# Attention with stacked high and low halves, moved weight splits, and grouped edge strips

## Chip, core and metric

The kernel runs on one core of a Trainium2 chip. The metric is the device time of one launch in microseconds (us), as the median of several runs. TensorE (PE), VectorE (DVE), ScalarE (ACT), GpSimd (POOL) and the DMA queues work from queues of their own, in order, and meet at semaphores.

## What is computed

Two graph layers over 625 nodes of width 768, with 10000 edges. The change touches three parts: the edge counts, and the linear attention of either layer.

```python
# layer 0, no softmax: q, k, v from xn @ W_qkv + b_qkv, 12 heads of 64
phi_q = relu(einsum('bhnd,md->bhnm', q, random_features))     # 256 features
phi_k = relu(einsum('bhnd,md->bhnm', k, random_features))
kv = einsum('bhnm,bhnd->bhmd', phi_k, v)
attn = einsum('bhnm,bhmd->bhnd', phi_q, kv) / 256
# layer 1
phi(t) = exp(einsum('bhnd,md->bhnm', t, random_features) - 0.5 * sum(t * t)) / 16
out = einsum('bhnm,bhmd->bhnd', q_p, kv) / (einsum('bhnm,bhm->bhn', q_p, k_sum) + 1e-6)
# edges, sorted by dst: how many of each type lead from a node to a node
count[src, dst] += BASE ** edge_type
```

All products are made in float32 accuracy from pairs: a value is held as high (rounded to fp32r) and low (the rest), and a product is the sum of two or three matmuls.

## The kernel before

The program is a row of phases, each a block with one instruction list for each engine, and a barrier behind it. `phase_start` (0 to 68 us in the trace) loads the input, counts the edges and normalises x. `phase_attend` is the attention, called as m0 (68 to 288 us) and, with `second` true, as m1 (1103 to 1347 us). Between and behind them stand graph convolutions, a feed-forward layer and the mixture of experts (from about 1500 us), which the change leaves as they are.

**The edge counts.** The 10000 edges are 80 tiles of 125. For tile n, `hot(n)` makes on DVE a one-hot matrix of the sources (`src_hot`, 125x640, L1204) and one of the destinations (`dst_hot`, L1206), which holds only a window of 96 columns, since the edges are sorted; the latter carries the weight of the edge type. TensorE multiplies them into PSUM (L1289, about six matmuls a tile). `src_hot` has 16 slots (UNROLL). DVE makes 24 tiles, then the statistics and the normalised x, and then the other 56. From tile 44 on, TensorE turns a piece of x every third tile (`turn`, L1273, ten pieces, all through bank 7): ACT copies the piece as high half (L1257), DVE subtracts for the low half (`low`, L1213), and only then the next piece may be turned. When all tiles are done, ACT and DVE copy the counts out of PSUM.

**The weight ring.** Weights arrive in chunks in a ring of two slots. `ring_high` (ACT, L128) rounds a chunk of 128x1536, `ring_low` (DVE, L139) makes the low half, and only then the slot of raw data takes the next load.

**The attention.** It begins with the values of all heads (`values`, L179), each tile of which DVE adds a bias to in m0 (L703), and the first pair's projection. Then a loop over six pairs of heads. For pair p TensorE does, in this order:

- `features_k`: five tiles of keys (t), each three matmuls of 512 columns (high*high, high*low, low*high) against `rfbd`, the random features of both heads in a block diagonal, and behind each tile one of twelve units of the next pair's projection (`project_unit`, L187, six matmuls of 314 columns; units 0 to 5 make keys, 6 to 11 queries). In m1 two further matmuls a tile subtract the squares (L477).
- `features_q`: four tiles of queries (m), six matmuls of 314 columns each, and behind each a unit. In m1 four more a tile.
- `keys_values` (L520), 40 matmuls; units 9 to 11; `attend`, 24 matmuls.

ACT makes the high half of each feature tile (L628, L641), DVE the low half (L747, L755; L745, L753 in m1). Tile t of the keys waits for the low half of tile t-2 in m0 and for the high half in m1, since they share a bank; so do the query tiles. `qk_high` and `qk_low` split the projected keys and queries, 128x628 at a time. The keys of the next pair are split behind the first query tile. At the end of a pair's pass stand, on ACT and DVE, the split of a ring chunk, in m0 the addition of `b_proj` to x (L788), and in m1 the reciprocal of the denominators, 128x628 on DVE (L781), and the product with it.

## Time and profile before

| what | us |
|---|---|
| median of 3 runs (2268.36 to 2272.95) | 2268.71 |
| the profiled execution | 2272.92 |
| its span | 2271.2 |
| DVE busy (58% of the span) | 1313.0 |
| PE busy (91% of the span) | 2067.2 |
| ACT busy (39% of the span) | 888.4 |

Busy time is the time in which an engine has an instruction under way. The profiled execution lies 4.2 us above the median. In the page's 40 slices of 56.8 us, PE is at five tenths in the first slice and at seven to nine in the next four, which are the start and the first attention.

### The profile page before, as it was taken

How to read it: one execution, taken by the hardware profiler on the slowest of the kernel's cores; microseconds unless marked ns; L12 is line 12 of the kernel's file. 1: busy time of each engine (PE TensorE's matmuls, PEld its weight loads, DVE VectorE, ACT ScalarE, POOL GpSimd, SP SyncE). 2: the span in 40 equal slices, each digit the busy share in tenths (PEclk: the TensorE clock that was granted, in tenths of full speed). 3: DMA queues.
4: the chain of work that ended last, by engine and by line, in shares of the span. 5: the costliest groups of instructions: out<-in, count | busy, mean ns of one | idle time of the engine just before them, and what ended most of it. 6: DMA issues, size and time to landing. Idle time of an engine off the chain costs nothing. (4 is left out here: it accounts for less than half of the span.)

```text
span 2271.2 us, 34213 instructions
## 1 busy us (share of the span) xinstructions
PE 2067.2 (91%) x13755; PEld 1941.2 (85%) x13755; DVE 1313.0 (58%) x1909; ACT 888.4 (39%) x1079; POOL 90.5 (4%) x60
## 2 busy tenths in 40 slices
PE   5799889999999999974799979699979999999996
PEld 4788879999999999974789979699978888888885
DVE  9444466433243434355545555663258888898896
ACT  1233331211111211211255542221237777777775
POOL 0000000000000000000010100000000110101001
PEclk8899989999999999986799988899989999999998
DMA  2310026210221111101210021231259999999997
GB/s 65 100 43 29 1 78 151 66 41 25 66 66 50 45 63 55 45 15 28 91 29 29 15 84 63 79 123 63 77 189 388 385 377 379 364 373 378 363 378 269
DMA packets 186157, 313.72 MB, mean 138 GB/s; under 512 B 12641, under 2 KB 86884, under 8 KB 185628
## 3 DMA queue, kind: packets, MB, share of 16 engines
q1 hardware_dynamic: 178844, 294.53, 36.9%
q0 software_dynamic: 4816, 16.62, 3.1%
q8 instruction: 88, 1.44, 0.3%
q10 hardware_dynamic: 2384, 0.92, 0.2%
q14 instruction: 25, 0.20, 0.0%
HBM read 293.56 MB, written 20.40 MB: 138 GB/s over the span
## 5 line engine op out<-in xcount | busy, mean ns | idle before, releaser
L179 PE MATMUL psum<-re_whi,xt_sb 128*128 128x512 f32 (+1 forms) x1680 | 507.9, 377 | 1.5 <-DVE xt_sb L2716 1.5
L179 PE MATMUL psum<-ring_hi,xt_sb 128*128 128x256 f32 (+3 forms) x1980 | 371.5, 286 | 14.1 <-DVE a_sb L703 6.0
L179 PEld LDWEIGHTS psum<-re_whi,xt_sb 128*128 128x128 f32 x1680 | 313.3, 189 | 46.7 <-issue 1.9
L179 PEld LDWEIGHTS psum<-ring_hi,xt_sb 128*128 128x128 f32 (+1 forms) x1980 | 314.1, 191 | 15.6 <-DVE a_sb L703 6.8
L2700 DVE TENSOR_TENSOR re_wlo<-moe_raw,re_whi 128x1536 fp32r<-128x1536 f32 x173 | 303.5, 1756 | 35.2 <-ACT re_whi L2654 34.5
L179 PE MATMUL psum<-re_wlo,xt_sb 128*128 128x512 f32 (+1 forms) x840 | 313.6, 373 | 0.0
L2654 ACT ACTIVATE re_whi<-moe_raw 128x1536 fp32r<-128x1536 f32 x174 | 258.6, 1489 | 91.0 <-PE psum L179 87.6
L179 PE MATMUL psum<-ring_lo,xt_sb 128*128 128x256 f32 (+3 forms) x990 | 281.9, 285 | 0.0
L179 PEld LDWEIGHTS psum<-ring_lo,xt_sb 128*128 128x128 f32 (+1 forms) x990 | 189.4, 191 | 0.0
L179 PEld LDWEIGHTS psum<-re_wlo,xt_sb 128*128 128x128 f32 x840 | 159.1, 189 | 21.9
L128 ACT ACTIVATE ring_hi<-ring_raw 128x1536 fp32r<-128x1536 f32 (+2 forms) x67 | 102.3, 1526 | 176.7 <-PE psum L187 81.4
L139 DVE TENSOR_TENSOR ring_lo<-ring_raw,ring_hi 128x1536 fp32r<-128x1536 f32 (+2 forms) x67 | 121.8, 1818 | 75.7 <-ACT ring_hi L128 66.1
L2700 DVE TENSOR_TENSOR re_wlo<-re_more,re_whi 128x1536 fp32r<-128x1536 f32 x84 | 147.6, 1758 | 29.7 <-ACT re_whi L2654 29.7
L179 PE MATMUL psum<-ring_hi,gnn_sb 128*128 128x256 f32 (+1 forms) x810 | 150.6, 287 | 7.2 <-PEq L1308 4.2
L2654 ACT ACTIVATE re_whi<-re_more 128x1536 fp32r<-128x1536 f32 x84 | 125.2, 1490 | 41.3 <-PE psum L179 37.6
L187 PE MATMUL psum<-xt_sb,ring_hi 128*128 128x314 f32 x744 | 140.7, 312 | 0.0
L1458 DVE TENSOR_TENSOR g_y<-psum,g_y 128x256 fp32r<-128x256 f32 (+3 forms) x105 | 42.4, 405 | 167.8 <-ACT g_y L1425 167.6
L179 PEld LDWEIGHTS psum<-ring_hi,gnn_sb 128*128 128x128 f32 (+1 forms) x810 | 127.4, 190 | 9.0 <-issue 7.8
L1425 ACT ACTIVATE g_y<-psum 128x256 fp32r<-128x256 f32 (+3 forms) x105 | 38.6, 368 | 232.1 <-PE psum L179 232.1
L187 PEld LDWEIGHTS psum<-xt_sb,ring_hi 128*128 128x128 f32 x744 | 119.8, 192 | 4.7
L1401 PE MATMUL psum<-gnn_sb,g_y 128*128 128x314 f32 (+1 forms) x780 | 117.1, 308 | 0.0
L179 PE MATMUL psum<-ring_lo,gnn_sb 128*128 128x256 f32 (+1 forms) x405 | 115.6, 285 | 0.0
(391 smaller groups left out, 3282.8 us busy)
## 6 DMA issues: line engine op xcount, KB each, us to landing
moe_raw<-in_L_ffn_Wg_r SPq DMA_DIRECT2D x74, 768.0 KB, 8.6
moe_raw<-in_L_ffn_Wu_r SPq DMA_DIRECT2D x58, 768.0 KB, 8.3
moe_raw<-in_L_ffn_Wd_r SPq DMA_DIRECT2D x42, 768.0 KB, 6.0
re_more<-in_L_ffn_Wd_r SPq DMA_DIRECT2D x42, 768.0 KB, 9.2
re_more<-in_L_ffn_Wu_r SPq DMA_DIRECT2D x30, 768.0 KB, 7.6
ring_raw<-in_L_gnn_w_rel SPq DMA_DIRECT2D x18, 896.0 KB, 5.0
re_more<-in_L_ffn_Wg_r SPq DMA_DIRECT2D x15, 768.0 KB, 7.1
ring_raw<-in_L_mix_W_qkv SPq DMA_DIRECT2D x24, 384.0 KB, 4.3
```

The source lines that it names most:

```text
L128: act.activation(ring.hi[:, g % RING_SLOTS, 0:size], ring.raw[:, g % RING_SLOTS, 0:size], ACT.Copy).then_inc(ring.hi_done, 1)
L139: dve.tensor_tensor(lo, raw, hi.bitcast(F32), ALU.subtract).then_inc(ring.lo_done, 1)
L179: mm = pe.matmul(out, lhs[a], rhs[b], start=(first and i == 0), stop=(last and i == 2))
L187: mm = pe.matmul(bank_pair[:, h, 0:HN], lhs[a], rhs(b, h), start=(first and i == 0), stop=(last and i == 2))
L1401: mm = pe.matmul(pair[:, h, 0:HN], y[0:TS[t], v % 2, t, a, m * P:(m + 1) * P], k.C[0:TS[t], r, t, h * HN:(h + 1) * HN], start=(t == 0 and ...
L1425: act.activation(y[0:TS[t], v % 2, t, 0, 0:w], k.banks[i % 3][0:TS[t], 0:w], ACT.Copy).then_inc(s["y_hi"], 1)
L1458: dve.tensor_tensor(y[0:TS[t], v % 2, t, 1, 0:w], k.banks[i % 3][0:TS[t], 0:w], y[0:TS[t], v % 2, t, 0, 0:w].bitcast(F32), ALU.subtract).t ...
L2654: act.activation(whi[:, slot, :], raw[i % RAWS], ACT.Copy).then_inc(s["hi_done"], 1)
L2700: dve.tensor_tensor(wlo[:, i % RING, :], raw[i % RAWS], whi[:, i % RING, :].bitcast(F32), ALU.subtract)\
```

## The change

**Stacked halves.** `qk` gets a slot for each head. For head hd the partitions of that head hold the high half, and the other 64 partitions hold the low half of the same head. `rf2` holds the features twice, one below the other, as high (index 0) and low (index 1), 256 columns each. A matmul over 128 partitions then sums high and low of q or k at once. A key tile takes four matmuls of 256 columns, a query tile four of 314. `qk_high` and `qk_low` are two instructions of 64 partitions each where one of 128 stood.

**Order in a pair's pass.** Unit 5 goes ahead of the query tiles, and so does the split of the next keys. The ring's split goes from the end of a pass to behind the query tiles of the next one, and with it in m0 the addition of `b_proj`. In m1 the reciprocal of pair p-1 is made in four parts of 157 columns behind the first four key tiles of pair p, and the product follows the split of the keys; the wait for the squares stands ahead of a key tile.

**The start.** `phase_start` loads the three biases and the features for m0, behind chunk 0. The destination one-hots are made for eight tiles in one `tensor_tensor` (125x768, window starts on a straight line for eight tiles, from POOL's iota), and the weight goes to the source side. Every fourth source one-hot is made on ACT, in two steps: |column - source|, and relu(weight - weight * that).

```diff
-            bv = k.sb(f"{name}_bv", [P, D], F32)
-            bq = k.sb(f"{name}_bq", [P, 2 * PAIRS], F32)
-            bp = k.sb(f"{name}_bp", [P, D], F32)
+            bv, bq, bp = k.v_bias, k.qk_bias, k.out_bias
...
-                    mm = split_product(pe, out, [qk[:, KEYS, a, t * P:t * P + TS[t]] for a in range(2)],
-                                       [rfbd[:, a, :] for a in range(2)], True, not second)
+                    for hd in range(2):
+                        out = key_bank(t)[:, hd * MF:(hd + 1) * MF]
+                        for a in range(2):
+                            mm = pe.matmul(out, qk[:, KEYS, hd, t * P:t * P + TS[t]], rf2[:, a, :],
+                                           start=(a == 0 and not second), stop=(a == 1 and (hd == 1 or not second)))
                     mm.then_inc(s["pk_mm"], 1)
                     project_unit(p + 1, t)
+                project_unit(p + 1, TT)
...
-                    mm = split_product_wide(pe, pair, [rfbd[:, a, m * P:(m + 1) * P] for a in range(2)],
-                                            lambda b, h: qk[:, QUERIES, b, h * HN:(h + 1) * HN], True, not second)
+                    hd, e = divmod(m, 2)
+                    for a in range(2):
+                        for h in range(2):
+                            mm = pe.matmul(pair[:, h, 0:HN], rf2[:, a, e * P:(e + 1) * P],
+                                           qk[:, QUERIES, hd, h * HN:(h + 1) * HN],
+                                           start=(a == 0), stop=(a == 1 and not second))
...
+                for hd in range(2):
+                    src, dst = qk_pair[a][own(hd), :, 0:HN], halves(qk[own(hd), a, hd, :])
...
+                if p + 1 < PAIRS:
+                    qk_high(p + 1, KEYS)
                 for m in range(4):
...
-                    if m == 0 and p + 1 < PAIRS:
-                        qk_high(p + 1, KEYS)
...
+                if p >= 1 and p + 5 <= len(st.chunks):
+                    ring_high(act, st, p + 5)
                 act.wait_ge(s["kv_mm"], p + 1)
...
-            if not second:
-                dve.wait_ge(s["bias_in"], 32)
...
+                    if second and p >= 1 and t < 4:
+                        quarter = den[:, t * (NT // 4):(t + 1) * (NT // 4)]
+                        if t == 0:
+                            dve.wait_ge(s["den_f"], 2 * p)
+                        ins = dve.reciprocal(quarter, quarter)
...
+                if p + 1 < PAIRS:
+                    qk_low(p + 1, KEYS)
+                if second and p >= 1:
+                    normalise(p - 1)
...
+GROUP = 8
+ON_ACT = [n for n in range(ET) if n % 4 == 3]
...
+            def strips(g):
+                at = slice(g * GROUP, (g + 1) * GROUP)
+                columns = iota[0:EP, 0:WINDOW].rearrange("p (o w) -> p o w", o=1).broadcast_to([EP, GROUP, WINDOW])
+                places = within[:, at].rearrange("p (j o) -> p j o", o=1).broadcast_to([EP, GROUP, WINDOW])
+                dve.tensor_tensor(dst_hot[:, at, :], columns, places, ALU.is_equal).then_inc(s["strip"], 1)
...
+                act.activation(away[:, i % 2, :], iota[0:EP, :], ACT.Abs, bias=minus[:, 0, n:n + 1]).then_inc(s["away"], 1)
+                act.wait_ge(s["away"], i + 1)
+                act.activation(src_hot[:, n % UNROLL, :], away[:, i % 2, :], ACT.Relu, bias=weight[:, 0, n:n + 1],
+                               scale=minus[:, 1, n:n + 1]).then_inc(s["act_hot"], 1)
```

How the instructions stand on DVE in m0, before, over one pass of a pair (p = 1: L747 is the low half of key tiles, L755 of query tiles, L718 the low half of the projected keys or queries, L139 the ring):

```order
L747 SCALAR_TENSOR_TENSOR m_phik<-psum,m_phik 113x512
L755 SCALAR_TENSOR_TENSOR m_phiq<-psum,m_phiq 128x628
L718 SCALAR_TENSOR_TENSOR m_qk<-psum,m_bq,m_qk 128x628
L755 SCALAR_TENSOR_TENSOR m_phiq<-psum,m_phiq 128x628 x3
L766 SCALAR_TENSOR_TENSOR m_kvf<-psum,m_kvt 128x2x64 x2
L773 TENSOR_TENSOR m_kv<-m_kvf,m_kv 128x512
L718 SCALAR_TENSOR_TENSOR m_qk<-psum,m_bq,m_qk 128x628
L139 TENSOR_TENSOR ring_lo<-ring_raw,ring_hi 128x1536
L788 TENSOR_TENSOR x_sb<-x_sb,m_bp 128x768
L747 SCALAR_TENSOR_TENSOR m_phik<-psum,m_phik 128x512 x4
```

The same place on DVE in the changed kernel (L752 key tiles, L771 query tiles, L720 projected keys or queries):

```order
L752 SCALAR_TENSOR_TENSOR m_phik<-psum,m_phik 113x512
L720 SCALAR_TENSOR_TENSOR m_qk<-psum,qk_bias,m_qk 64x628 x2
L771 SCALAR_TENSOR_TENSOR m_phiq<-psum,m_phiq 128x628 x4
L139 TENSOR_TENSOR ring_lo<-ring_raw,ring_hi 128x1536
L777 TENSOR_TENSOR x_sb<-x_sb,out_bias 128x768
L784 SCALAR_TENSOR_TENSOR m_kvf<-psum,m_kvt 128x2x64 x2
L791 TENSOR_TENSOR m_kv<-m_kvf,m_kv 128x512
L720 SCALAR_TENSOR_TENSOR m_qk<-psum,qk_bias,m_qk 64x628 x2
L752 SCALAR_TENSOR_TENSOR m_phik<-psum,m_phik 128x512 x4
```

The ring and the addition have gone from ahead of the key tiles to behind the query tiles, and the split of the next keys from behind the first query tile to ahead of it.

DVE in m1 of the changed kernel, from the numerators of pair 0 (L797) to the query tiles of pair 1 (L750 key tiles, L758 the reciprocal, L726 the product with it):

```order
L797 COPY a_sb<-psum 64x628 x2
L750 TENSOR_TENSOR m_phik<-x_sb,m_phik 128x512
L758 RECIPROCAL x_sb<-x_sb 128x157
L750 TENSOR_TENSOR m_phik<-x_sb,m_phik 128x512
L758 RECIPROCAL x_sb<-x_sb 128x157
...
L750 TENSOR_TENSOR m_phik<-x_sb,m_phik 113x512
L718 TENSOR_TENSOR m_qk<-psum,m_qk 64x628 x2
L726 TENSOR_TENSOR a_sb<-a_sb,x_sb 128x628
L769 TENSOR_TENSOR m_phiq<-x_sb,m_phiq 128x628 x4
L139 TENSOR_TENSOR ring_lo<-ring_raw,ring_hi 128x1536
```

And before:

```order
L779 COPY a_sb<-psum 64x628 x2
L781 RECIPROCAL x_sb<-x_sb 128x628
L783 TENSOR_TENSOR a_sb<-a_sb,x_sb 128x628
L139 TENSOR_TENSOR ring_lo<-ring_raw,ring_hi 128x1536
L745 TENSOR_TENSOR m_phik<-x_sb,m_phik 128x512 x4
```

The reciprocal, the product and the ring all stood ahead of the first key tile; now one part of the reciprocal stands behind each of the first four.

## Rows read from the trace of the kernel before

**Rows 1.** Stretches: us, busy time (instructions) per engine, granted clock, DMA share, GB/s
```profile
178.90:264.50 85.60, 78.73 (x527) 75.67 (x526) 36.83 (x49) 30.79 (x48) 0.00 (x0) 0.98 0.06 19
1183.80:1311.40 127.60, 123.34 (x805) 115.65 (x805) 72.38 (x84) 71.88 (x120) 12.40 (x8) 1.00 0.06 19
```

**Rows 2.** Timeline, DVE, first tiles: start us, us, engine, line, operation [idle before]
```profile
6.74 0.39 DVE L1204 TENSOR_SCALAR n_src_hot<-n_iota,n_edges_f 125x640 bf16<-125x640 f16 x1
7.04 0.30 DVE L1206 TENSOR_SCALAR n_dst_hot<-n_iota,n_edges_f,n_edge_weight 125x96 bf16<-125x96 f16 x1
7.26 0.38 DVE L1204 TENSOR_SCALAR n_src_hot<-n_iota,n_edges_f 125x640 bf16<-125x640 f16 x1
```

**Rows 3.** Timeline, start, where x is turned between edge tiles
```profile
57.08 0.63 PE L1273 MATMUL psum<-ident,n_xn 128*128 128x128 f32 x4 [0.77 <-DVE xt_sb L1213]
...
57.74 0.60 ACT L1257 ACTIVATE xt_sb<-psum 128x512 fp32r<-128x512 f32 x1 [1.70 <-PE psum L1273]
...
58.37 0.69 DVE L1213 TENSOR_TENSOR xt_sb<-psum,xt_sb 128x512 fp32r<-128x512 f32 x1
...
59.21 0.41 PE L1273 MATMUL psum<-ident,n_xn 128*128 128x128 f32 x2 [0.83 <-DVE xt_sb L1213]
...
64.43 0.40 DVE L1213 TENSOR_TENSOR xt_sb<-psum,xt_sb 128x226 fp32r<-128x226 f32 x1
```

**Rows 4.** Timeline, the first values of m0
```profile
79.08 1.76 DVE L139 TENSOR_TENSOR ring_lo<-ring_raw,ring_hi 128x1536 fp32r<-128x1536 f32 x1 [9.37 <-DMA m_bq<-in_L_mix_b_qkv]
...
81.23 0.58 PE L179 MATMUL psum<-ring_hi,xt_sb 128*128 128x256 f32 x1 [5.81 <-DVE a_sb L703]
...
81.61 0.42 PE L179 MATMUL psum<-ring_lo,xt_sb 128*128 128x256 f32 x1
...
82.25 0.41 PE L179 MATMUL psum<-ring_lo,xt_sb 128*128 128x256 f32 x1
...
85.06 0.28 PE L179 MATMUL psum<-ring_lo,xt_sb 128*128 128x256 f32 x1
...
85.42 0.28 PE L179 MATMUL psum<-ring_lo,xt_sb 128*128 128x256 f32 x1
```

**Rows 5.** Timeline, PE and DVE in passes of m0
```profile
163.04 1.04 PE L187 MATMUL psum<-m_qk,m_rfbd 128*128 128x314 f32 x6
...
164.79 1.04 PE L187 MATMUL psum<-m_qk,m_rfbd 128*128 128x314 f32 x6
...
168.30 4.58 PE L520 MATMUL psum<-m_v,m_phik 128*128 128x130 f32 x40
...
178.95 0.85 PE L179 MATMUL psum<-m_rfbd,m_qk 128*128 128x512 f32 x3
...
179.64 0.74 PE L187 MATMUL psum<-xt_sb,ring_hi 128*128 128x314 f32 x4
...
181.25 1.76 DVE L139 TENSOR_TENSOR ring_lo<-ring_raw,ring_hi 128x1536 fp32r<-128x1536 f32 x1 [3.98 <-ACT ring_hi L128]
...
182.93 0.95 DVE L788 TENSOR_TENSOR x_sb<-x_sb,m_bp 128x768 f32<-128x768 f32 x1
...
184.53 0.96 PE L179 MATMUL psum<-m_rfbd,m_qk 128*128 128x512 f32 x3 [2.30 <-DVE m_phik L747]
```

**Rows 6.** The tile m_qk: duration in ns, least/median/most, first and last start
```profile
L587 ACT ACTIVATE m_qk<-psum,m_bq x12: 783/785/787, 106.0 to 261.2; 128x628 fp32r<-128x628 f32 x12
L718 DVE SCALAR_TENSOR_TENSOR m_qk<-psum,m_bq,m_qk x12: 871/872/875, 106.8 to 262.0; 128x628 fp32r<-128x628 f32 x12
L583 ACT ACTIVATE m_qk<-psum x12: 693/696/702, 1132.6 to 1307.7; 128x628 fp32r<-128x628 f32 x12
```

**Rows 7.** Timeline, passes of m1: reciprocal, and waits of the key tiles
```profile
1184.77 4.08 DVE L781 RECIPROCAL x_sb<-x_sb 128x628 f32<-128x628 f32 x1
...
1188.57 0.96 PE L179 MATMUL psum<-m_rfbd,m_qk 128*128 128x512 f32 x3 [0.59 <-ACT m_phik L628]
...
1319.17 0.95 PE L179 MATMUL psum<-m_rfbd,m_qk 128*113 128x512 f32 x3 [1.88 <-ACT m_phik L628]
```

203 lines of the change are left out of this document (127 added, 76 removed).

## The prediction

> **What bounds the kernel now.** I read the busy time by stretches first, to see which engine sets the pace where the change works, and then the timeline of one pass. In both attention loops it is PE: three passes of the first attention (m0) take 85.6 us with PE busy for 78.7, four of the second (m1) 127.6 us with PE busy for 123.3, while DVE and ACT are busy for little over half of that at most [rows 1]. So a matmul taken away there is worth its time, and in m0 PE's idle time, 2.3 us a pass, is worth more still. The timeline says what it waits for: the third key tile waits for the low half of the first (at 184.53) [rows 5], and DVE made that late, since the ring's split (from 181.25) and the addition of b_proj (182.93) stood ahead of it. The start is another matter. There DVE works without a gap on one-hots, and PE waits for it. A tile costs DVE 0.30 us for the source part and 0.22 for the window (the starts at 6.74, 7.04 and 7.26) [rows 2], 0.52 together. And m0 begins with a hole: PE idles for 5.81 us until DVE has taken the first values away, DVE having waited 9.37 us for a bias to land [rows 4].
>
> **The start.** DVE's work for the tiles: 60 source parts at 0.30 are 18.0 us, and ten strips of 768 elements. No row has such a strip. The nearest is the addition of two 128x768 tiles, 0.95 us (at 182.93) [rows 5]; neighbours on DVE overlap by some 0.08 us (the 1.76 us at 181.25 are followed after 1.68), so ten strips cost 8.7 us. Bounds: 3 us, were a strip no dearer than a source part of nearly the same size, and 12, were broadcast operands dear. Before, the tiles took 80 x 0.52 = 41.6 us; now 26.7. But the end of this stage does not follow DVE alone. From tile 44 on there is a chain over ten pieces of x: PE turns (57.08), ACT copies 0.66 later, DVE subtracts 0.63 later, PE turns the next 0.84 later [rows 3], 2.1 us for a large piece and by the smaller shapes about 1.5 for a small one. It went at (64.43 - 58.37) / 3 = 2.0 us a piece, with one-hots in between. Now ACT also has 20 source parts to make, of two dependent instructions each. The nearest rows are activations of 628 elements, 0.70 us without a bias read per partition and 0.79 with one [rows 6]; the first step has one such operand and the second two, so 0.80 + 0.88, some 1.7 us a tile. Eight of them fall among the ten pieces. ACT's copies take 5 x 0.60 + 5 x 0.38 (the latter scaled down from 512 to 256 elements) = 4.9 us, the eight tiles 13.6, and for the two pieces that have no tile ahead of them the chain shows, about 2.5: 21 us from the first piece to the last one-hot, against 9 x 2.0 + 1 before. So nothing is gained behind tile 44, and perhaps 2 us lost. Ahead of it ACT is not late: it makes six tiles while DVE makes the first 24, and the rest while DVE does the statistics. DVE gains there on 24 + 29 tiles: 53 x 0.52 = 27.6 us before, 40 x 0.30 + 7 x 0.87 = 18.1 now, less 0.5 for four small instructions ahead of the first tile. In all 27.6 - 18.1 - 0.5 - 2 = 7, and since the last tiles no longer wait for DVE, I take **8 us** (3 to 13). The four small loads stand on SP's queue ahead of chunk 1, which nobody needs for 40 us. POOL's ten iotas stand ahead of the identity matrix; at a tenth of a microsecond each they are hidden behind the edges' landing, and I leave them in the range.
>
> The Trainium skill speaks against giving ACT this work. ScalarE: Activation LUTs, in its Rules for kernel authors, says to put relu and its like on VectorE, which is faster per element in bf16. The rows agree as to the price, 0.30 us against an estimated 1.7, and what counts here is only whose queue is free.
>
> **The hole at the head of m0.** With the bias there beforehand, DVE takes the values as they come and PE does not stop: 5.8 us. Behind the hole the clock was low. Three matmuls of 256 columns took 0.64 us at 81.61 and 0.36 at 85.06 [rows 4], which is the step from the level of 1.2 GHz to that of 2.4, and this lasted from 81.2 to 84.4: half of 3.2 us, 1.6. **7.5 us** (5.5 to 9). The memory transfers that the next chunks need begin as before, at the barrier; the ring is not the cover of anything new.
>
> **m0, a pass.** A key tile's three matmuls of 512 columns took 0.69 us (178.95 to 179.64). Four of 256 take 4 x 0.118 = 0.47 [rows 4]: 0.22 less, 1.1 for five tiles. A query tile with its unit took 1.75 us for twelve matmuls of 314 columns (163.04 to 164.79), 0.146 each; two less in each of four tiles is 1.2. Together **2.3 us**. Should matmuls of 256 columns cost as much as those of 314, the weights being changed each time, the key tiles would gain only 0.5. The wait of 2.3 us goes, since the ring and the addition now stand where DVE waits for the 4.4 us of `keys_values` (168.30) anyway: ACT's part of the split and then 1.7 + 0.9 on DVE end about when PE is through, so this cover is just wide enough; were it not, the remainder would fall on the path up to `attend`. With the wait goes a part of the clock's dips (0.98 in the mean) [rows 1], 0.8 a pass. What is late next: the query tiles. Unit 5 done, ACT makes two high halves of 0.79, and DVE then two low halves of 0.87, at which only it starts on the low half of query tile 0 (another 0.8). That is 0.2 + 1.5 + 1.6 + 0.8 = 4.1 us behind unit 5. PE does two query tiles with their units in 2 x (4 x 0.146 + 0.875) = 2.9 and then needs it: a new wait of **1.3 us**, in five passes, where it had none. It is bounded by 0.5 (if neighbours overlap more than I take) and 1.8. A pass gains 2.3 + 2.3 + 0.8 - 1.3 = 4.1. Four such passes give 16.4. The first one had another wait, on the ring split ahead of the loop, which stays and even grows as PE is sooner there: 0.6. The last has no units to fill the gaps and is paced by DVE: 1.0. **m0's loop: 18 us** (13 to 24).
>
> **m1, a pass.** The same 2.3 from the matmuls. The waits are smaller: 0.59 us for the third key tile (at 1188.57) [rows 7], and (127.6 - 123.3) / 4 = 1.1 in all [rows 1]. The ring's conversion on ACT, which caused the 0.59, goes behind the query tiles; I give 1.0 for the waits. Doubling the splits costs nothing here, as PE waits in m1 for high halves only. DVE is the one to watch: a quarter of the reciprocal is 4.08 / 4 = 1.02 us and a key tile 0.65 (0.87 for 628 elements [rows 6], scaled to 512, less the overlap), together 1.7, against PE's 0.47 + 2 x 0.23 + 0.875 = 1.8 for a key tile with its unit. It just fits. Four passes: 4 x 3.3 = 13.2. The first, which had no wait, gains 1.9. The last has nothing to hide behind; DVE's 4.08 in one piece made PE wait, once for 1.88 us [rows 7], and in quarters it will wait less: 2.0 (0 to 4). Ahead of the loop the split of the queries now takes ACT and DVE 0.6 and 0.7 us longer and PE already waits there: -0.9. **m1: 16 us** (10 to 20).
>
> **The sum.** 8 + 7.5 + 18 + 16 = 49.5 us. The profiled execution took 2272.9, which gives 2223.4; it lies 4.2 above the median of the three runs, and so I forecast 2268.7 - 49.5 = 2219. The rest of the kernel stands behind barriers and is moved as a whole.
>
> **Rivals.** (a) DVE becomes the bound in m1. If a quarter costs 1.3 us rather than 1.02, a key tile costs DVE 2.0 against PE's 1.8; ACT waits for the low half two tiles back, PE for ACT, and a pass loses 0.2 x 5 and the waits that I struck, 1.8 in all. Over five passes 9 us: 2228. For it: DVE is at 57% of m1's passes already and gets 1.4 us more a pass. Against: the reciprocal's time goes with its elements. (b) The start gains nothing, since ACT's one-hots hold the chain (2.5 us a tile instead of 1.7 would do): 2227. (c) More is gained: the new wait in m0 is absent because the instructions overlap, the last passes and the start are at the good end of their ranges: 9 us more, 2210. (d) Slower. PE's clock fell to the low level around the 5.81 us hole and in m0's passes of which the wait was 2.3 (0.98). If the new wait at the third query tile, 1.3 us, let it fall there and it stayed so to the end of the pass, then 2.9 + 4.4 + 2.6 + 3.5 = 13.4 us of matmuls would take twice as long, 67 us over five passes: 2286, 0.8% slower. From a cost of 10 us a pass on this decides the sign. Against it: after a wait as long as 2.3 us the mean clock was still 0.98.
>
> TensorE: Matmul & The Clock Gate, in the Trainium skill, describes under HAM oscillation a kernel that idled for a transfer in every step and started each step at the low clock; that is mechanism (d), which this trace shows behind a hole of 5.8 us and barely in the passes.
>
> **How the numbers follow.** The forecast, within 2213 to 2225: 52%. (a) 16%, (b) 11%, (c) 19%, (d) 2%. The range must reach (a), (b) and (c) with their spread: 2207 to 2231. A measurement of this kernel can tell 0.2% from no change, 4.5 us. Faster by more than that is all but (d) and a little beside it: 97%; within it 1%; slower 2%.
>
> **What would show it.** The strip's and ACT's durations, and the start of the count copies at about 57 us instead of 65.4. No wait of PE at the third tile of m0's values. Key tiles of four matmuls at 0.47 us. In m0 no wait at the third key tile, but one of 1.3 us at the third query tile for DVE's low half. Passes of 24.7 us in m0 and 28.5 in m1. Wrong would be: waits of PE for DVE in m1's key tiles (a), turns more than 2.3 us apart (b), or a clock under 0.9 in the passes (d).

## The result: 38 us faster, 12.6 us above the forecast time

| | before | after | difference |
|---|---|---|---|
| median, us (executions) | 2269.89 (4) | 2231.60 (4) | 38.3 |
| lowest to highest | 2268.36 to 2272.95 | 2230.74 to 2233.24 | |
| ratio, 95% interval | | 0.9830 (0.9813 to 0.9848) | |
| profiled execution / its span | 2272.9 / 2271.2 | 2230.7 / 2229.0 | 42.2 |

The forecast was 2219 (2207 to 2231), so the time came out 12.6 us above the forecast and 0.6 us above the range. The sign was right, the size was not: 49.5 us forecast, 42.2 found between the two profiled executions, 38.3 between the medians. Where the 42.2 come from shows in a table by stages, made from PE's timelines: the first matmul of m0, the first key tile of each pass, the first matmul of the phase behind each attention.

| stage, us | before | after | gain | forecast |
|---|---|---|---|---|
| start, to m0's first matmul | 68.2 | 62.4 | 5.8 | 8 |
| m0 ahead of its loop | 53.8 | 46.4 | 7.4 | 7.5 |
| m0 pass 1 | 27.3 | 28.7 | -1.3 | 0.6 |
| m0 passes 2 to 5 | 115.2 | 99.3 | 15.9 | 16.4 |
| m0 pass 6, to the next phase | 25.8 | 24.7 | 1.1 | 1.0 |
| m1 ahead of its loop | 49.7 | 50.8 | -1.1 | -0.9 |
| m1 pass 1 | 30.9 | 29.5 | 1.4 | 1.9 |
| m1 passes 2 to 5 | 127.6 | 115.1 | 12.5 | 13.2 |
| m1 pass 6, to the next phase | 37.9 | 37.8 | 0.2 | 2.0 |
| all other phases | | | 0.3 | 0 |

Four parts of it are short: the start (2.2 us), m0's first pass (1.9), m1's last pass (1.8) and m1's passes 1 to 5 (1.2). The other 5 us of the 12.6 are in the base: I took a gain worked out on a profiled execution from the median of others, 4.2 us below it, and the profiled execution after the change lies 0.9 below its own median.

The trace of the changed kernel, in the order of the rows shown of before. A stretch answers to each of [rows 1]: us, PE's busy time, granted clock, DMA share, GB/s; first passes 2 to 5 of m0, then pass 6 of m0, passes 2 to 5 of m1, pass 6 of m1.

```profile
137.44:236.72 99.28, 93.74 (x690) 1.00 0.09 25
236.72:261.39 24.67, 15.94 (x102) 0.92 0.02 2
1155.16:1270.26 115.10, 113.09 (x793) 1.00 0.07 21
1270.26:1308.02 37.76, 23.19 (x126) 0.79 0.02 6
```

PE is busy 94% of m0's passes 2 to 5, where it was 92% in [rows 1], and at full clock. Against [rows 2] stand the groups of the start by shape (times, mean ns after the bar): the source one-hots with their second operation, a strip, and the two steps on ACT.

```profile
L1240 DVE TENSOR_SCALAR n_src_hot<-n_iota,n_edges_f,n_edge_weight 125x640 bf16<-125x640 f16 x60 | 22.8, 441 | 0.0
L1247 DVE TENSOR_TENSOR n_dst_hot<-n_iota,n_within 125x768 bf16<-125x768 f16 x10 | 9.5, 951 | 0.0
L1309 ACT ACTIVATE n_src_hot<-n_away,n_edge_weight,n_minus 125x640 bf16<-125x640 f16 x20 | 18.4, 920 | 0.7
L1307 ACT ACTIVATE n_away<-n_iota,n_minus 125x640 f16<-125x640 f16 x20 | 16.3, 817 | 7.4 <-DVE n_minus L1276 5.2 <-PE psum L1367 2.3
```

Against [rows 4 and 5], PE's timeline (start, us, ..., [idle before]): m0's first matmuls with no hole, pass 1, the second pass's first key tile.

```profile
62.38 0.36 PE L179 MATMUL psum<-ring_hi,xt_sb 128*128 128x256 f32 x1 [2.78 <-PEq L1174]
...
63.05 0.60 PE L179 MATMUL psum<-ring_hi,xt_sb 128*128 128x256 f32 x2
...
113.67 0.75 PE L476 MATMUL psum<-m_rf,m_qk 128*128 128x256 f32 x4 [2.06 <-DVE m_phik L752]
114.25 1.22 PE L187 MATMUL psum<-xt_sb,ring_hi 128*128 128x314 f32 x4
...
124.66 0.85 PE L502 MATMUL psum<-m_qk,m_rf 128*128 128x314 f32 x4 [1.38 <-DVE m_phiq L771]
...
137.44 0.64 PE L476 MATMUL psum<-m_rf,m_qk 128*128 128x256 f32 x4
137.91 0.74 PE L187 MATMUL psum<-xt_sb,ring_hi 128*128 128x314 f32 x4
```

A key tile takes 0.47 us (137.44 to 137.91), as forecast, and the wait at the third query tile is 1.38 us, in each of five passes, where 1.3 was forecast. Two things were not priced. At 63.05 the matmuls take longer (the low clock, 63.05 to 66.2). And behind the wait of the third key tile of pass 1, 2.06 us, the next four matmuls take 1.22 us instead of 0.74: the granted clock is 0.57 from 114 to 118 us, where it was 1.00 in the first pass before. DVE's timeline names what is ahead of that key tile:

```profile
111.25 1.76 DVE L139 TENSOR_TENSOR ring_lo<-ring_raw,ring_hi 128x1536 fp32r<-128x1536 f32 x1 [0.95 <-ACT ring_hi L128]
112.93 1.28 DVE L752 SCALAR_TENSOR_TENSOR m_phik<-psum,m_phik 128x512 fp32r<-128x512 f32 x2
```

That is the split of chunk 5, which the change left ahead of the loop. A third thing stands ahead of m0's loop, DVE and PE:

```profile
98.23 1.75 DVE L720 SCALAR_TENSOR_TENSOR m_qk<-psum,qk_bias,m_qk 64x628 fp32r<-64x628 f32 x2 [3.48 <-ACT m_qk L589]
100.02 1.76 DVE L139 TENSOR_TENSOR ring_lo<-ring_raw,ring_hi 128x1536 fp32r<-128x1536 f32 x1
101.81 0.76 DVE L703 TENSOR_TENSOR a_sb<-psum,v_bias 128x256 f32<-128x256 f32 x2
102.29 0.38 PE L179 MATMUL psum<-ring_hi,xt_sb 128*128 128x256 f32 x1 [1.44 <-DVE a_sb L703]
```

PE waits 1.44 us there for values that DVE takes away only behind the split, now of two instructions, and a ring chunk. The kernel before has no such wait. The last pass of m1, against [rows 7], DVE, ACT and PE:

```profile
1277.35 1.12 DVE L758 RECIPROCAL x_sb<-x_sb 128x157 f32<-128x157 f32 x1
...
1278.93 1.12 DVE L758 RECIPROCAL x_sb<-x_sb 128x157 f32<-128x157 f32 x1
1280.09 0.69 DVE L750 TENSOR_TENSOR m_phik<-x_sb,m_phik 113x512 fp32r<-113x512 f32 x1
...
1280.89 0.69 ACT L644 ACTIVATE x_sb<-psum 128x628 f32<-128x628 f32 x1 [2.29 <-DVE m_phik L750]
...
1282.22 1.41 PE L502 MATMUL psum<-m_qk,m_rf 128*128 128x314 f32 x4 [2.14 <-ACT m_phiq L645]
...
1286.58 5.48 PE L526 MATMUL psum<-m_v,m_phik 128*128 128x130 f32 x40
```

The quarters stand between DVE's key tiles, which end at 1280.8; ACT waits 2.29 us for that, PE 2.14 for ACT, and the clock falls behind it (1.41 us for four matmuls that take 0.73 at full clock).

### The profile page after: what moved, and what is told of

It is laid out like the page before. It is cut to its first block and busy times, and to the rows that moved or that the text cites. A ratio compares the mean times of both kernels' runs of the same rounds, so it can differ in the third digit from the quotient of the medians.

```text
span 2229.0 us, 34175 instructions
## 1 busy us (share of the span) xinstructions
PE 2031.5 (91%) x13715; PEld 1919.2 (86%) x13715; DVE 1324.0 (59%) x1860; ACT 940.3 (42%) x1143; POOL 89.9 (4%) x70
## 3 DMA queue, kind: packets, MB, share of 16 engines
q8 instruction: 88, 1.44, 0.3%
## 5 line engine op out<-in xcount | busy, mean ns | idle before, releaser
L139 DVE TENSOR_TENSOR ring_lo<-ring_raw,ring_hi 128x1536 fp32r<-128x1536 f32 (+2 forms) x67 | 121.5, 1813 | 56.2 <-ACT ring_hi L128 56.0
```

What stands on the lines that cost most here:

```text
L139: dve.tensor_tensor(lo, raw, hi.bitcast(F32), ALU.subtract).then_inc(ring.lo_done, 1)
```

## Experiments

Each is timed beside executions of the kernel before, whose median lies between 2268.5 and 2272.4 us from one group of runs to the next, so that the ratios compare better than the times. The stage times are of the profiled execution of each; the profile's stages agree from kernel to kernel within 0.2 us where nothing was changed and the clock is full.

### The three parts alone

Each takes one part of the change into the kernel before: the counts of the start; the four small loads moved to the start; the attention. The fourth is the change whole, once more.

> The kernel before with the new counting of the first stage alone (grouped edge strips, every fourth source one-hot on ScalarE); biases and both attentions are the old ones. Theory (the stages add up): the first matmul of m0 starts near 62.4 instead of 68.1 us and everything behind keeps its length, so the time falls by 5.5 to 6.5 us (ratio 0.9974). Rival (the loads that m0 waits for at its head start in m0 and not earlier, but the weights it streams were asked for in the first stage and now have 6 us less to land): part of the 5.8 us comes back as a longer wait in the first 54 us of m0, and the time falls by only 2 to 4 us.

> The kernel before with the four small loads of m0 (three biases and the random features) moved into the first stage alone. Theory: the hole at the head of m0 goes and nothing else moves: the stretch from m0's first matmul to its first pass falls from 53.8 to about 46.4 us, and the time by 7 to 8 us (ratio 0.9967). Rival (part of the 7.4 us seen in the changed kernel came from its other edits, such as the smaller feature matrix, or the first stage pays for the four loads): under 5 us.

> The kernel before with the new attention alone in both layers (stacked halves, the new order of ScalarE and VectorE, reciprocal in quarters); first stage old, biases loaded in m0. Theory: passes 2 to 5 take 24.8 us each in m0 and 28.8 in m1, a wait of 1.38 us stands at the third query tile of each of the first five passes of m0, the wait of about 2.1 us at the third key tile of m0's first pass is there too, since both come from the order on VectorE; the time falls by 25 to 30 us (ratio 0.988). Rival (the late third key tile of the first pass and the low clock behind it come from the earlier start of m0): pass 1 is 26.8 us or less here against 28.7 in the changed kernel, and the time falls by 28 to 32.

> The changed kernel once more, beside the three parts on one chip. Theory: the three parts make the whole: 0.9974 * 0.9967 * 0.988 = 0.982 of the kernel before. Rival (they interact): the whole differs from the product by over 0.2%. It also tells how the executions of the kernel before scatter about the profiled one, of which about 4 us of the miss are made.

| | median | ratio (95%) | m0 starts | ahead of loop | m0: pass 1, 2 to 5 (mean), 6 | m1: pass 1, 2 to 5, 6 |
|---|---|---|---|---|---|---|
| before | 2269.7 | | 68.2 | 53.8 | 27.3, 28.8, 25.8 | 30.9, 31.9, 37.9 |
| start_only | 2265.6 | 0.9979 (0.9970 to 0.9989) | 62.2 | 54.0 | 27.4, 28.8, 25.8 | 31.0, 31.9, 38.0 |
| bias_only | 2258.2 | 0.9944 (0.9927 to 0.9961) | 68.2 | 43.6 | 27.3, 28.8, 27.0 | 30.9, 31.9, 36.8 |
| attend_only | 2244.8 | 0.9889 (0.9873 to 0.9905) | 69.5 | 55.9 | 28.7, 24.9, 25.4 | 29.5, 28.7, 36.2 |
| same_after | 2232.0 | 0.9826 (0.9811 to 0.9842) | 62.8 | 47.5 | 28.7, 24.8, 25.5 | 29.6, 28.8, 37.7 |

The theory of added stages holds for the start (6.0 us in the trace, 4.1 between medians; the head of m0 keeps its length, so the rival of a longer wait there is out) and the attention (24.9 us; pass 1 has its 28.7 here too, so the rival that the earlier start made it late is out). It fails for the biases: alone they bring 10.3 us ahead of the loop, not 7.4, and 11.5 between medians. The three medians' gains add up to 40.4 us, the whole has 37.7; by the ratios this is 0.9813 for the product and 0.9826 (0.9811 to 0.9842) for the whole, so the times alone don't tell them apart, and the stages have to. Ahead of m0's loop bias_only takes 43.6 us, the changed kernel 46.4, and two things make these 2.8 us. One is the wait of 1.44 us at 102.29: attend_only has it too, 1.44 us, and order_only (below), with the new order but splits of one instruction, does not, so the doubled splits bring it. The other is the clock. PE's stretches show it, 10 us from m0's first matmul on (busy, clock, DMA share, GB/s): before, bias_only, after; then the first 7 us of before and of bias_only.

```profile
68.00:78.00 10.00, 7.24 (x36) 0.67 1.06 292
```
```profile
68.00:78.00 10.00, 9.82 (x83) 1.00 1.03 319
```
```profile
62.00:72.00 10.00, 9.62 (x69) 0.83 1.01 312
```
```profile
68.00:75.00 7.00, 6.82 (x34) 0.55 1.00 299
```
```profile
68.00:75.00 7.00, 6.82 (x57) 1.00 1.00 315
```

So before, the clock was low ahead of the hole as well, and not only behind it, and bias_only gains that too. What lets it be high there is not shown. With the old start it was 0.55 from 68 to 75 us in two profiles, 0.76 in two more, and 1.00 in bias_only alone; with the new start and no matmuls added there, all eleven profiles that have the early biases show 0.50 to 0.64 from 62 to 66 us.

### What the order is worth and what the matmuls

order_only has the new order and the quarters with the old products of three matmuls; old_order is the changed kernel with the old order of ACT and DVE. The core of order_only, on DVE (old_order goes the other way):

```diff
                     ins.then_inc(s["pk_lo"], 1)
...
+                if p + 1 < PAIRS:
+                    qk_low(p + 1, KEYS)
...
                 for m in range(4):
...
-                    if m == 0 and p + 1 < PAIRS:
-                        qk_low(p + 1, KEYS)
+                if p >= 1 and p + 5 <= len(st.chunks):
+                    ring_low(dve, st, p + 5)
...
-                if p + 6 <= len(st.chunks):
-                    ring_low(dve, st, p + 6)
```

> The kernel before with the new order on ScalarE, VectorE and TensorE and the reciprocal in quarters, but with the old feature products of three matmuls (no stacked halves), the old first stage and the biases loaded in m0. Theory (the order takes the waits away, the stacked halves 2.33 us of matmuls from each pass, and in m0 the wait of 1.38 is less here, since the first two query tiles are 0.3 us longer each): passes 2 to 5 take 26.3 to 26.8 us in m0 and 30.5 to 31.2 in m1; against the kernel before the time falls by 10 to 16 us. Rival (the two parts only help together, as the stacked halves did harm with the old order: 29.3 to 34 us a pass in m0 against 28.0 and 29.6 before): passes within 0.5 us of before.

> The changed kernel with the stacked halves but the old order on ScalarE and VectorE: keys of the next pair behind the first query tile, weight split at the end of the pass, reciprocal whole at the end. Theory (of the 4.1 us per pass gained in m0, 2.3 are matmuls and 1.8 the order net of its new wait): passes 2 to 5 of m0 take 26.3 to 26.8 us each, no wait of 1.38 us; those of m1 29.8 to 31.0; the time rises by 10 to 16 us against the changed kernel. Rival (the order brings nothing net, the matmuls and the clock that stays up do it all): within 3 us of the changed kernel.

order_only: 2253.2 us, 0.9921 (0.9905 to 0.9937); passes 2 to 5 take 25.45 to 25.49 us in m0, where I expected 26.3 to 26.8, and 30.5 in m1, with no wait in m0's. old_order: 2255.8 us (2246 to 2272), 0.9930 (0.9910 to 0.9950), 24 us slower than the changed kernel, m0's passes 33.1, 34.0, 29.3, 30.4, 30.5 us in the profiled execution, which is the slowest of its six. I expected 26.3 to 26.8 a pass and a loss of 10 to 16, so both missed. m1's passes came as expected, 30.5 us. With shorter key tiles PE comes to the third one sooner, and the old order makes it wait longer than the old products did: 2.97 us here, 2.30 in [rows 5].

```profile
178.25 1.76 DVE L139 TENSOR_TENSOR ring_lo<-ring_raw,ring_hi 128x1536 fp32r<-128x1536 f32 x1 [2.39 <-ACT ring_hi L128]
179.93 0.95 DVE L791 TENSOR_TENSOR x_sb<-x_sb,out_bias 128x768 f32<-128x768 f32 x1
```
```profile
181.63 0.74 PE L476 MATMUL psum<-m_rf,m_qk 128*128 128x256 f32 x4 [2.97 <-DVE m_phik L752]
182.21 0.93 PE L187 MATMUL psum<-xt_sb,ring_hi 128*128 128x314 f32 x4
...
184.31 1.25 PE L187 MATMUL psum<-xt_sb,ring_hi 128*128 128x314 f32 x4
```

The low clock behind it does the rest (0.93 and 1.25 us for what takes 0.74). So in m0 the stacked halves, 2.3 us of matmuls a pass, bring 0.65 with the new order (25.47 to 24.82). The new wait takes the rest: 1.38 us of idling, and 1.65 with the slower start behind it (172.49 to 175.01 us from one unit to the next at the third query tile, 171.03 to 171.90 at the second). With the old order they do harm in m0 (29.3 to 34.0 us a pass against 28.0 to 29.6 before), but not in m1, where a pass takes 30.5 us against 31.9 before.

### The new wait in m0

q_first puts the keys' low half behind the first query tile on DVE. interleave puts the low half of one head there where it was, and that of the other behind the second query tile, ACT signalling the heads apart:

```diff
-                if p + 1 < PAIRS:
-                    qk_low(p + 1, KEYS)
+                if p + 1 < PAIRS:
+                    qk_low(p + 1, KEYS, range(2) if second else (0,))
...
                     ins.then_inc(s["pq_lo"], 1)
+                    if not second and m == 1 and p + 1 < PAIRS:
+                        qk_low(p + 1, KEYS, (1,))
```

> The changed kernel; on VectorE, in m0 alone, the low half of the first query tile is taken ahead of the low half of the next pair's keys. Theory (the 1.38 us at the third query tile are the two instructions of the keys' low half, which stand ahead of it): the wait goes in all five passes, nothing takes its place, passes 2 to 5 take 23.4 to 23.6 us instead of 24.8, and the time falls by 6 to 7 us against the changed kernel. Rival (ScalarE or the key-value bank is next: it waits for the keys' low half or for the later low halves): a wait of 0.5 us or more appears ahead of the key-value product or at the fourth query tile, and only 2 to 4 us are gained.

> The changed kernel; ScalarE signals the two halves of the split keys apart, and VectorE in m0 takes the low half of one head ahead of the first query tile and that of the other behind the second. Theory (moving the whole 1.75 us pair of instructions behind the first tile only moved the wait, 0.31 + 0.90 us at the third and fourth query tile in place of 1.38, since both tiles' low halves have to be there in time): of the 1.38 us 0.2 to 0.4 stay at the third tile, none at the fourth, passes 2 to 5 take 23.7 to 24.0 us, and five passes bring 4.5 to 6 us. Rival (the key-value product then waits for the second head's low half): 0.5 us or more ahead of that product, passes 24.3 or more.

q_first: 2228.9 us, 0.9819 (0.9802 to 0.9836); passes of 24.93, nothing gained there (its median is 3 us under same_after's, the interval reaches over that). The wait was moved, not removed: the two low halves of the keys (1.75 us) now stand ahead of the second tile's, which the fourth needs.

```profile
149.56 0.85 PE L502 MATMUL psum<-m_qk,m_rf 128*128 128x314 f32 x4 [0.31 <-DVE m_phiq L771]
...
152.19 0.85 PE L502 MATMUL psum<-m_qk,m_rf 128*128 128x314 f32 x4 [0.90 <-DVE m_phiq L771]
```

interleave: 2225.9 us, 0.9804 (0.9784 to 0.9823); passes of 23.74 to 23.78 us, one wait of 0.33, and in m1 28.3 instead of 28.7, which I had not expected; I put it down to DVE starting one ACT instruction sooner there too, and did not test it alone.

```profile
171.93 0.85 PE L502 MATMUL psum<-m_qk,m_rf 128*128 128x314 f32 x4 [0.33 <-DVE m_phiq L772]
```

### The first pass of m0 and the last of m1

ring_later drops the split of chunk 5 ahead of the loop and lets the first pass make it behind its query tiles, as the others do. last_half takes, in m1's last pass alone, two quarters behind the query tiles.

```diff
-                if p >= 1 and p + 5 <= len(st.chunks):
+                if p + 5 <= len(st.chunks):
```
```diff
-                    if second and p >= 1 and t < 4:
+                    if second and p >= 1 and t < (4 if p + 1 < PAIRS else 2):
...
+                if second and p == PAIRS - 1:
+                    link(dve.reciprocal(den[:, NT // 2:NT], den[:, NT // 2:NT]))
+                    normalise(p - 1)
```

> The changed kernel; the split of weight chunk 5 stands no longer ahead of the first pass of each attention but behind the query tiles of that pass. Theory (the 2.06 us wait at m0's third key tile, and the low clock behind it, come from the 1.76 us of this split on VectorE): pass 1 of m0 takes 25.2 to 26.2 us instead of 28.7, that of m1 falls by up to 0.6, and the time falls by 2.5 to 4 us. Rival (the low clock there doesn't depend on the wait): pass 1 keeps its slow matmuls near 114 us and gains 2 us at most.

> The changed kernel; in the last pass of m1 alone two of the four reciprocal quarters stand as one half behind the query tiles, with the multiplication that uses them. Theory (the four quarters delay VectorE, then ScalarE, then the third query tile by 2.14 us, and the clock falls behind that wait): the last pass takes 35.3 to 36.3 us instead of 37.8, and the time falls by 1.5 to 2.5 us. Rival (the half of 2.1 us then delays the key-value result on VectorE): the gain at the query tiles is given back ahead of the last attend, 0 to 0.5 us.

ring_later: 2223.7 us, 0.9795 (0.9777 to 0.9813); m0's pass 1 takes 24.8 us (it was 28.7) and m1's 28.65 (29.5). 3.9 us, so 2.06 of wait and the clock behind it were one thing. The stages show this gain; by ratio its interval still touches that of same_after (from 0.9811). last_half: m1's last pass takes 34.5 us (37.8), more than the wait of 2.14, for the same reason. Its median is 2227.3, 0.9818 (0.9800 to 0.9835), which the intervals do not tell from the changed kernel. In the profiled execution (2230.8 us) m0's last pass took 31.3 us, against 24.7, and that cost more than m1's gain. Two other executions of the same code of m0's last pass, same_after and last_half:

```profile
248.68 4.58 PE L526 MATMUL psum<-m_v,m_phik 128*128 128x130 f32 x40
255.70 5.28 PE L187 MATMUL psum<-m_phiq,m_kv 128*128 128x314 f32 x24 [2.45 <-DVE m_kv L791]
```
```profile
248.35 8.63 PE L526 MATMUL psum<-m_v,m_phik 128*128 128x130 f32 x40
259.43 6.27 PE L187 MATMUL psum<-m_phiq,m_kv 128*128 128x314 f32 x24 [2.44 <-DVE m_kv L794]
```

This matters beyond last_half. Ten profiles here have the changed kernel's code of m0's last pass: five took 24.7 to 25.5 us in it and five 30.6 to 31.3. The five profiles with the old products took 25.8 to 27.0. So the 24.7 us of the profiled execution were the lucky half.

### The price of the second operation, and the last tile

weight_on_wide moves, in the kernel before, the multiplication by the weight from the narrow one-hot to the wide one. act_earlier gives ACT tiles 2, 6, ... 78 instead of 3, 7, ... 79.

```diff
-                dve.tensor_scalar(src_hot[:, u, :], iota[0:EP, :], edges_f[:, 0, n:n + 1], None, ALU.is_equal)
+                dve.tensor_scalar(src_hot[:, u, :], iota[0:EP, :], edges_f[:, 0, n:n + 1], weight[:, 0, n:n + 1],
+                                  ALU.is_equal, ALU.mult)
```

> The kernel before; in the first stage the multiplication with the edge's weight is moved from the narrow destination one-hot (96 columns) to the wide source one-hot (640 columns), nothing else. Theory (the second operation costs 54 ns on 640 columns, 441 against 387, and this is what made the start gain 5.8 and not 8 us): the source one-hots take 441 ns, the narrow ones get at most 20 ns shorter, and the 80 tiles of the first stage end 2.7 to 4.3 us later. Rival (the price of an instruction there is not set by its number of operations but by what runs beside it, ScalarE's one-hots in the changed kernel above all): 387 ns stay and the stage ends within 1 us of before.

> The changed kernel with ScalarE making the source one-hots of tiles 2, 6, 10, ... 78 and not 3, 7, ... 79, so that the last tile of all is VectorE's. Theory (the last tile waits 0.85 us for ScalarE's second half): that wait goes, VectorE's last one-hot comes 0.4 us later than its last did, and m0 starts 0.4 to 0.8 us earlier. Rival (the chain of the turned tiles holds the end): no change, within 0.2 us.

```profile
L1204 DVE TENSOR_SCALAR n_src_hot<-n_iota,n_edges_f,n_edge_weight 125x640 bf16<-125x640 f16 x80 | 35.1, 439 | 0.0
L1207 DVE TENSOR_SCALAR n_dst_hot<-n_iota,n_edges_f 125x96 bf16<-125x96 f16 x80 | 19.2, 240 | 0.0
```

Before, these were 387 and 309 ns. So the price is 52 ns on the wide one and 69 on the narrow one: it does not grow with the width here, the pair costs 0.51 us either way, and the time is the same, 1.0005 (0.9992 to 1.0019). The theory was right on the 441 ns and wrong on the sum. m0 starts at 69.4 us in this profile, 1.2 later than before; attend_only, whose start is the old one, has 69.5, so this is no sign of a cost. act_earlier gained nothing (2233.5 us; m0 starts at 62.7): 0.71 of the 0.85 us of waiting for ACT stay, now at tile 78, whose two steps (57.55 and 58.40) ACT makes behind its share of the turned x.

### The clock

The last two passes have no next pair to project, and PE waits in them. fill_last puts matmuls there whose result nobody reads; fill_start adds one matmul of zeros, on one row, behind each of the tiles 48 to 78 of the start.

```diff
+            def fill(n):
+                for i in range(n):
+                    pe.matmul(qk_pair[QUERIES][:, i % 2, 0:HN], rf2[:, 0, 0:P], qk[:, QUERIES, 0, 0:HN],
+                              start=True, stop=True)
...
+                if p == PAIRS - 1:
+                    fill(14)
                 attend(p)
```
```diff
+                if 48 <= n < ET - 1:
+                    pe.matmul(k.banks[n % 7][:, 0:256], zeros[:, 0:P], zeros[:, 0:256], start=False, stop=False,
+                              skip_group_check=True)
```

> The changed kernel with matmuls that only keep TensorE busy (128x314, their result is read by nobody) in the last pass of both attentions, where there is no next pair to project: four behind the second and fourth key tile (in m0 and m1) and behind two of the query tiles, fourteen ahead of the last attend. They stand where the engine waited 0.8 to 2.9 us. Theory (the last pass of m0 takes 24.7, 25.5 or 31.3 us by chance of the clock, which falls in those waits: its key-value product takes 4.58 or 8.63 us and its attend 5.28 or 6.3 instead of 3.7): with the waits filled the clock stays at 1.00, the last pass of m0 takes 23 to 24 us in every execution and that of m1 1.5 to 3 us less, and the time falls by 4 to 8 us. Rival (the clock falls for another reason, or the added work delays the tiles as much as it saves): the last passes are within 1 us of before, or longer.

> The changed kernel with one matmul of zeros (1x128 by 1x256, added to a count bank, which changes nothing) behind each of tiles 48 to 78 of the first stage, 31 in all. Theory (m0's first 46.4 to 47.5 us would be 43.6, as with the biases alone, but for a low clock in their first 3 to 10 us, which follows a thinly used TensorE at the end of the first stage): the clock is 1.00 from m0's first matmul on, those 46.4 us fall to 43.5 to 44.5, and the time by 2 to 4 us. Rival (TensorE then becomes the bound of the first stage, or the clock falls all the same): m0 starts 1 us or more later, no gain.

fill_last: 2220.5 us, 0.9780 (0.9764 to 0.9796) against 0.9826 (from 0.9811) of same_after, which is 10 us. m0's last pass 23.1 us (24.7 to 31.3 without), m1's 33.3 (37.8); the attend behind fourteen added matmuls takes 3.76 us, not 5.28, and begins no later:

```profile
246.52 4.58 PE L538 MATMUL psum<-m_v,m_phik 128*128 128x130 f32 x40
250.94 2.25 PE L459 MATMUL psum<-m_qk,m_rf 128*128 128x314 f32 x14
253.55 3.76 PE L187 MATMUL psum<-m_phiq,m_kv 128*128 128x314 f32 x24 [0.36 <-DVE m_kv L805]
```

fill_start did the contrary of what I expected: 2242.7 us, 0.9884 (0.9865 to 0.9902), m0 starting at 75.5. Its rival was right in kind (the clock falls all the same, m0 starts later), but m0 starts 13 us later where it had said 1 or more. The clock fell about the first added matmul (41.1 us) and stayed at 0.50, the level of 1.2 GHz, to m0's start, with PE busy in the profile from 42 us to the last tile. improved joins the three edits that shortened their stages (ring_later, interleave, last_half); improved_fill adds the filling of fill_last; dense_full and zeros_full add 31 matmuls in the start to that, with all 125 rows, of dense values or of zeros:

> The changed kernel with three of the edits tried alone: weight chunk 5 split behind the first pass's query tiles, the keys' low halves of the two heads apart (the second behind the second query tile in m0), and two of the four reciprocal quarters behind the query tiles in the last pass of m1. Theory (they add up: 3.9 + 0.9, 5.2 + 2.3, 3.2 us): 15 us less in the stages, 2214 to 2219 us. Rival (with the waits in the passes gone the last pass of m0 falls into the low clock more often): 6 us of that come back in most executions, 2220 us or more.

> The same with the filling matmuls in the last passes of both attentions. Theory: both gains add up and the last pass no longer scatters: 2208 to 2214 us, and the executions lie closer together than those of the kernel without filling. Rival: no better than it, within 0.1%.

> The kernel improved_fill with, in the first stage behind each of tiles 48 to 78, one matmul 125x128 by 125x256 of the column numbers (dense values, all 125 rows), whose result goes to columns that nobody reads. In fill_start 31 matmuls of zeros on one row brought the clock down to 0.50 from 45 to 72 us, although TensorE was busy 10 of 10 us. Theory (a matmul of few rows or of zeros does not count as work for the clock, a dense one on all rows does): the clock stays at 0.83 or more in the first stage and at 1.00 from m0's first matmul on, m0 starts within 0.5 us of 62.4 and its first 46 to 47 us fall to 43.5 to 44.5; the time is 2205 to 2207 us. Rival (any added matmul there brings the clock down): m0 starts at 70 us or later, 2216 us or more.

> As dense_full, but the 31 matmuls multiply the tile's source one-hot (125 rows) by zeros (125x256). It tells the rows from the data. If the one row was what let the clock fall in fill_start, this kernel stays at 0.83 or more like dense_full. If it was the zeros, the clock falls to 0.50 as in fill_start and m0 starts near 75 us, 2220 us or more.

| | median | ratio (95%) | m0 starts | ahead of loop | m0: passes 1 to 5, 6 | m1: passes 1 to 5, 6 |
|---|---|---|---|---|---|---|
| improved | 2216.0 | 0.9757 (0.9739 to 0.9776) | 62.0 | 46.8 | 23.8, 30.6 | 28.3, 34.8 |
| improved_fill | 2208.2 | 0.9733 (0.9718 to 0.9748) | 62.6 | 47.0 | 23.8, 23.2 | 28.3, 32.5 |
| dense_full | 2208.7 | 0.9720 (0.9706 to 0.9735) | 62.0 | 44.6 | 23.8, 23.2 | 28.3, 32.5 |
| zeros_full | 2204.6 | 0.9710 (0.9694 to 0.9727) | 62.0 | 44.7 | 23.8, 23.1 | 28.3, 32.5 |

PE in the same stretches of fill_start, improved_fill and zeros_full (busy time, clock):

```profile
45.00:55.00 10.00, 10.00 (x76) 0.50 0.01 2
62.00:72.00 10.00, 10.00 (x85) 0.50 0.01 2
```
```profile
45.00:55.00 10.00, 6.06 (x101) 0.96 0.01 2
62.00:72.00 10.00, 9.37 (x59) 0.70 0.98 304
```
```profile
45.00:55.00 10.00, 7.80 (x124) 1.00 0.01 2
62.00:72.00 10.00, 10.00 (x85) 1.00 1.03 317
```

With 31 matmuls on one row the clock was 0.50; with 31 on 125 rows in the same places, of dense values or of a one-hot and zeros, it was 1.00 from 35 us through the start and into m0, whose head is 2.3 us shorter for it. This is one profile of each. Zeros in one operand are ruled out as the cause, but the rows are not shown to be it alone: in fill_start both operands are zeros, and no run has that on 125 rows. The head's 44.7 us in zeros_full, at full clock, are bias_only's 43.6 and the wait for DVE, 1.18 us there. Their times come 0.13 to 0.23% below improved_fill's by ratio, with intervals that overlap, so this last gain is shown by the stages and only suggested by the times. improved and improved_fill are shown faster than the changed kernel: their intervals end at 0.9776 and 0.9748, that of same_after begins at 0.9811.

## Why the forecast missed, point by point

**The start: 5.8 for 8.** The strip (0.95 us) and ACT's two steps (0.82 + 0.92) cost what I took. Failed: "60 source parts at 0.30". The change moves the multiplication onto them, and I priced them by the row without it; they take 441 ns and stand 0.36 apart. Over the 40 that count ahead of the turns that is 2.4 us. The trace agrees: DVE comes to the first piece of x 6.3 us sooner (39.57 for 45.91), where the terms had 9.0. Behind it two smaller errors cancel in part. The chain, priced at a loss of 2 us, lost nothing (its last low half 6.8 us sooner, 57.60 for 64.43), and the last tile, which I had waiting for nobody, waits 0.85 us for ACT's one-hot. So 5.8 are left. That the second operation costs its 0.05 to 0.07 us at either width, so that it weighs on whatever part is left, weight_on_wide shows.

**The head of m0: 7.5 found as 7.4, and for half the reason.** The hole's 5.8 us are gone. But the low clock did not cost 1.6 in all: before, it stood at 0.55 from 68 to 75 us too, ahead of the hole, where I had not looked, and bias_only shows the whole to be worth 10.3. On the other side 2.8 us came back. About half is the clock, low again from 63.05 to 66.2 us. The other half is the wait of 1.44 us for DVE: I had priced the doubled split of the queries ahead of the loop in m1 (-0.9) and put it at nothing in m0. Errors that cancel, so 7.4 for 7.5 is luck. The runs with filling on 125 rows show that the clock's part can be had.

**m0's loop: 15.7 for 18.** Passes 2 to 5 came within 0.5 us of the forecast, the new wait included (1.38 for 1.3, though 4.1 - 2.9 is 1.2). Failed: "The first one had another wait, on the ring split ahead of the loop, which stays and even grows as PE is sooner there: 0.6". I forecast a gain of 0.6 us for that pass and it lost 1.3. The wait grew from 1.58 to 2.06 us, much as I had it, and the clock fell behind it (0.57 for 4 us, some 1.7 us by that share), to which I gave nothing; ring_later took the two away together, 3.9 us. I had named the mechanism and not priced its second half. The last pass, 1.1 us found for 1.0, is luck: the same code took 24.7 to 31.3 us in other profiles, against 25.8 to 27.0 before.

**m1: 13.0 for 16.** The quarter of the reciprocal costs 1.12 us, not 1.02 (4 x 1.12 = 4.5 for 4.08). Rival (a) did not come about in passes 2 to 5, where key tiles do not wait for the feature tiles. It came about in the last pass, where no unit stands between the key tiles. Failed: "in quarters it will wait less: 2.0". The longest wait is 2.14 us where it was 1.88, now at the third query tile, and the clock falls behind it, so the pass gained 0.2. last_half returns 3.2 us of it. In the middle passes 0.2 us each are missing: waits of 0.27 to 0.45 stand at the start of a pass for DVE's copies, and interleave, where they are gone, gives 0.45 a pass back. That the doubled low half of the queries delays the copies is argued and not shown. (Rival (a)'s 1.8 us a pass should read 2.0: 0.2 x 5 and the 1.0 of waits.)

**The base.** I set a sum made on the profiled execution (2272.9) against the median of three (2268.7). The executions of the kernel before now known by the rounds lie between 2261 and 2276, their medians between 2268.5 and 2272.4. What made the profiled one slow is not shown: two of its four middle passes of m0 took 29.6 us and two 28.0, but so did those of start_only, bias_only and weight_on_wide. On the other side, the profiled execution after the change has the short last pass of m0, which half the profiles of that code don't have. So the 42.2 us are more than a typical pair shows, and 38 is the better figure.

Rival (b) fell: the turns stand 2.14 us apart (37.19 to 56.46 in nine), where it would have decided above 2.3. The 2.0 us a piece that I read of before came from the last four pieces; over all ten it was 2.32 (42.23 to 63.14). Rival (d), the clock falling at the new wait, did not come about: 1.00 in passes 2 to 5. Its place was right in kind, though: waits of 2.06 and 2.14 us did bring the clock down in the first and the last pass, one of 1.38 did not.

The Trainium skill, in TensorE: Matmul & The Clock Gate, section What's actually happening, lets the clock follow how busy PE has been. fill_last agrees with that, 3.76 us for 5.28. fill_start does not, as the profile counts busy time, with PE busy 10.00 of 10.00 us at 0.50; there the measurement decides.

## What to carry to other kernels

A shorter instruction on the bounding engine pays only as far as its feeders keep up: reorder these first, then shorten (in m0 here 2.3 us of matmuls brought 0.65, and with the old order a loss). Price a wait with the clock behind it: taking away 2.06 us of wait brought 3.9, and 2.14 brought 3.2. Look at the passes at either end of a loop, which lack the work that hides things in the middle, and at the same instructions wherever else they stand, such as the doubled splits ahead of m0's loop. Where such a wait couldn't be removed, matmuls on all rows that nobody reads covered it here (fill_last, 10 us). And look at more than one profile before a stage's time is believed: the same last pass took 24.7 or 31.3 us.

## What the runs showed of the hardware

- Matmuls of one row (1x128 by 1x256, both operands zeros) behind each tile: clock 0.50 from 45 to 72 us with PE busy all the time. Matmuls of 125 rows in the same places: 1.00, for a one-hot and zeros as for dense values.
- The same 40 matmuls of 128x130 took 4.58 us at a granted clock of 1.00 (same_after) or 8.63 at 0.50 (last_half). How much of this kernel's scatter that makes was not separated.
- A second operation in a TENSOR_SCALAR on 16-bit elements cost 52 ns at 640 columns and 69 at 96.
- RECIPROCAL: 4.08 us for 628 columns, 2.11 for 314, 1.12 for 157, so nearly by the element.
